# Three gatings moved forward in VectorE's order and two squares moved between the tiles' signs, in a cross-attention and mixture-of-experts kernel

## The chip, the cores and the metric

The kernel runs on one core of a Trainium2 chip. The metric is the device time of one execution in microseconds, as the median of several executions; the times of the profile are microseconds from the start of the profiled span.

## What is computed

For each of 16 examples of 256 tokens and width 256 the reference adds a cross-attention over 77 context rows and then a mixture of experts, each behind a layer norm. The attention has 16 heads and uses sparsemax in place of softmax.

```python
x = x + xattn(layernorm(x), ctx, ctx, ...)
x = x + ffn(layernorm(x), ...)

# xattn, per head:
scores = einsum('bhqd,bhkd->bhqk', qh, kh) * scale
attn   = sparsemax(scores)             # max(scores - tau, 0), sums to 1
out    = einsum('bhqk,bhkd->bhqd', attn, vh) ... @ Wo + bo

# ffn:
_, idx = top_k(logits + lb_bias, 2);  w = sigmoid(sel_logits); w = w / (sum(w) + 1e-6)
hidden     = square(relu(einsum('nd,ehd->neh', xf, w1)))       # 8 experts
expert_out = einsum('neh,edh->ned', hidden, w2)
moe_out    = einsum('ned,ne->nd', expert_out, we)
shared     = square(relu(x @ cfc.T)) @ cproj.T
```

## The kernel before

The kernel is a software pipeline over examples. Each engine runs 19 turns, `b` from 0 to 18, and in turn `b` it works on four examples at four depths: *new* (example b: norm, queries, scores, first estimate of tau), *mid* (example b-1: the remaining rounds on tau), *late* (example b-2: attention product, output projection, second norm, routing) and *old* (example b-3: the experts). Turns 3 to 15 have all four; turn 16 has no new example, turn 17 only late and old, turn 18 only old. In turns 0 to 2 nothing is old. The order of the work inside a turn is written out by hand for each engine in its function `turn`. All engines wait on semaphores, and each runs its instructions strictly in the order written.

**The experts (old).** Nine of them, the shared one first. For the i-th, TensorE's `layer1` (L807) writes `h_ps` with eight matmuls; VectorE's `old_gates` (L1072), called as `gates(i)`, multiplies the rectified result by the square root of the routing weight into `g` (ScalarE does it for i = 0); ScalarE's `old_square` (L577), called as `square(i)`, squares `g` into `hid`; TensorE's `layer2` (L820) accumulates it into `y_ps`. `h_ps`, `g` and `hid` are double buffers: `layer1(i)` waits until gating i-2 is done, `gates(i)` waits for `layer1(i)` and for square i-2, and `layer2(i)` waits for square i.

**The rounds (new and mid).** A round r on tau is: GpSimd subtracts tau from the scores, one tile of 128 tokens at a time (L335, `over`); ScalarE takes the signs (L526) and the relu (L528), in `sign_relu`; VectorE's `newton` folds the signs (L945, `fold_a`), sums the relu (L948), both for two tiles, then folds again (L954), sums (L958), takes a reciprocal (L960), a step (L962) and the new tau (L966). A function `between` is called after the second fold. Round 0 and 1 belong to the new example, where round 1's `newton` comes at the head of the next turn; rounds 2 and 3 are mid's. Round 3 has no signs.

**Routing (late).** TensorE's output projection (L780) feeds VectorE's `late_stats` (L1035 and the statistics), then GpSimd's `late_rstd` (L406, L408), ScalarE's `late_norm` (L481), TensorE's transposes (L788) and logits (L796). At a turn's end GpSimd's `late_pick` and `late_weight_roots` (L417, a power) make the roots of the weights `sw`. TensorE's `late_roots` (L665) transposes `sw`, which is TensorE's last step of the turn; its next is `layer1(0)` of the next turn. From there `sw` goes by ScalarE and two transfers into `sw_all`, which `gates(1)` of the next turn reads.

On GpSimd, behind round 0's tau of the new example, stand in this order: `subtract(b, p, 1, 0)` (waits for that tau), `late_pick`, `subtract(b, p, 1, 1)`, `mid_verdict`, `late_weight_roots`. On TensorE, around the change, stand `new_scores(b, 1)` (L732, waits until ScalarE has copied the first tile's scores, L514 and L516), `l2(2)`, the first product (L762, L771), `l1(4)`, `l2(3)`, `l1(5)`, the second product, the output projection, `l2(4)`, `l1(6)`, `l2(5)`, the transposes of x1n, `l1(7)`, the logits, `l2(6)`, `l1(8)`, `l2(7)`, `l2(8)`, `late_roots`.

Of the kernel before, what the change touches and what calls it, by code (L numbers as in the profile page):

```python
# [64 lines left out]
def xattn_moe_kernel(nc, x, ctx_in, wq, wk, wv, wo, bq, bk, bv, bo, gate_w, lb_bias, w1, w2, cfc, cproj,  # L65
# [4 lines left out]
    with ExitStack() as stack:  # L70
# [134 lines left out]
        def rt(r, t):  # L205

            return r * T + t + 1
# [248 lines left out]
        def _(act):  # L456
# [122 lines left out]
            def turn(b, p, q, new=False, mid=False, late=False, old=False, ahead=True):  # L579
                def square(i):  # L580
                    if old and i == 0:
                        old_shared(b - 3)
                    if old:
                        old_square(b - 3, i)

                def keys_on(i):
                    if b < 2:
                        i += PAIRS // 2 * b
                        pair_keys(i)
                        if i < PAIRS - 1:  # L590
                            pair_context(i + 1)

                if b == 0:
                    pair_context(0)
                    pair_keys(0)
                if new:
                    new_turned(b, 0)
                square(0)
                if new:
                    new_turned(b, 1)  # L600
                    new_queries(b)
                square(1)
                if mid:
                    sign_relu(b - 1, q, 2, 0)
                    sign_relu(b - 1, q, 2, 1)
                if new:
                    new_scores(b, p, 0)
                square(2)
                if new:
                    new_scores(b, p, 1)  # L610
                if b == 0:
                    pair_context(1)
                if b == 1:
                    keys_on(0)
                if late:
                    late_product(b - 2, 0)
                square(3)
                if mid:
                    sign_relu(b - 1, q, 3, 0)
                    sign_relu(b - 1, q, 3, 1)  # L620
                if late:
                    late_product(b - 2, 1)
                square(4)
                if new:
                    sign_relu(b, p, 0, 0)
                    keys_on(1)
                    sign_relu(b, p, 0, 1)
                    keys_on(2)
                square(5)
                if late:  # L630
                    late_norm(b - 2, p)
                if late:
                    late_turned(b - 2, p)
                if mid:
                    mid_attention(b - 1, 0)
                square(6)
                if late:
                    late_sigmoids(b - 2)
                if mid:
                    mid_attention(b - 1, 1)  # L640
                square(7)
                if new and ahead:
                    new_norm(b + 1, q)
                keys_on(3)
                if new:
                    sign_relu(b, p, 1, 0)
                square(8)
                if new:
                    sign_relu(b, p, 1, 1)
                if late:  # L650
                    late_roots(b - 2)
# [239 lines left out]
        def _(dve):  # L891
# [32 lines left out]
                dve.wait_ge(top_chain.sem, top_chain.at(b, 2 * t + 1))  # L924
                dve.tensor_reduce(top_sum[:, t], top8[:, t], AX.X, ALU.add).then_inc(top_chain.sem, 1)

            def newton(b, p, r, between, gap=None):

                n0 = 4 * r
                if r == COUNTS:  # L930
                    for t in range(T):
                        dve.wait_ge(relu_done.sem, relu_done.at(b, rt(r, t)))
                        dve.tensor_reduce(fsum[:, t * NH:(t + 1) * NH], over[:, p, t], AX.X, ALU.add  # L933
                                          ).then_inc(f_summed.sem, 1)
                    between()
                    dve.wait_ge(f_summed.sem, f_summed.at(b))
                    dve.scalar_tensor_tensor(step[:], fsum[:], -1.0, rden[:], ALU.add, ALU.mult
                                             ).then_inc(newton_chain.sem, 1)
                    dve.wait_ge(newton_chain.sem, newton_chain.at(b))
                    dve.scalar_tensor_tensor(flat(tau[:, p]), step[:], 2.0, flat(tau[:, p]), ALU.mult, ALU.add  # L940
                                             ).then_inc(tau_ready.sem, 1)
                    return
                for t in range(T):
                    dve.wait_ge(sign_done.sem, sign_done.at(b, rt(r, t)))
                    dve.tensor_tensor(fold_a[:, t], signs[:, p, t, :, 0:SW // 2], signs[:, p, t, :, SW // 2:], ALU.add  # L945
                                      ).then_inc(signs_folded.sem, 1)
                    dve.wait_ge(relu_done.sem, relu_done.at(b, rt(r, t)))
                    dve.tensor_reduce(fsum[:, t * NH:(t + 1) * NH], over[:, p, t], AX.X, ALU.add  # L948
                                      ).then_inc(f_summed.sem, 1)
                    if gap is not None and t == 0:  # L950
                        gap()
                dve.wait_ge(signs_folded.sem, signs_folded.at(b, rt(r, 1)))
                halves = fold_a[:].rearrange("p t h k -> p (t h) k")
                dve.tensor_tensor(fold_b[:], halves[:, :, 0:SW // 4], halves[:, :, SW // 4:], ALU.add  # L954
                                  ).then_inc(newton_chain.sem, 1)
                between()
                dve.wait_ge(newton_chain.sem, newton_chain.at(b, n0 + 1))
                dve.tensor_reduce(den[:, p], fold_b[:], AX.X, ALU.add).then_inc(newton_chain.sem, 1)  # L958
                dve.wait_ge(newton_chain.sem, newton_chain.at(b, n0 + 2))
                dve.reciprocal(rden[:], den[:, p]).then_inc(newton_chain.sem, 1)  # L960
                dve.wait_ge(newton_chain.sem, newton_chain.at(b, n0 + 3))
                dve.scalar_tensor_tensor(step[:], fsum[:], -1.0, rden[:], ALU.add, ALU.mult  # L962
                                         ).then_inc(newton_chain.sem, 1)
                dve.wait_ge(newton_chain.sem, newton_chain.at(b, n0 + 4))

                dve.scalar_tensor_tensor(flat(tau[:, p]), step[:], 2.0, flat(tau[:, p]), ALU.mult, ALU.add  # L966
                                         ).then_inc(tau_ready.sem, 1)
# [114 lines left out]
            def turn(b, p, q, new=False, mid=False, late=False, old=False, ahead=True):  # L1082
                def gates(i):
                    if old:
                        old_gates(b - 3, q, i)

                def newton_and_gates(stage, b, p, r, i, gap=None):
                    if stage:
                        newton(b, p, r, lambda: gates(i), gap)
                    else:  # L1090
                        gates(i)

                def values(i):
                    if b < 2:
                        pair_values(PAIRS // 2 * b + i)

                def verdict():
                    if late:
                        late_verdict(b - 2)

                if mid:
                    newton(b - 1, q, 1, verdict)
                else:
                    verdict()
                gates(1)
                if new and ahead:
                    new_stats(b + 1, q)
                if late:
                    late_settle(b - 2, p)
                newton_and_gates(mid, b - 1, q, 2, 2)  # L1110
                if new:
                    new_tau(b, p, 0)
                gates(3)
                if new:
                    new_tau(b, p, 1)
                values(0)
                newton_and_gates(mid, b - 1, q, 3, 4)
                if mid:
                    mid_magnitude(b - 1, q)
                if late:  # L1120
                    late_stats(b - 2, p)
                gates(5)
                newton_and_gates(new, b, p, 0, 6, lambda: values(1))
                values(2)
                gates(7)
                if mid:
                    mid_tolerance_sum(b - 1)
                if late:
                    late_gate(b - 2)
                values(3)  # L1130
                if late:
                    late_weights(b - 2)
                gates(8)
                if old:
                    old_finish(b - 3, q)
# [30 lines left out]
```

## Time and profile before

| | |
|---|---|
| device time, median of 3 runs | 932.8 us (932.24 to 937.07) |
| profiled execution, own time | 933.74 us |
| its span | 931.9 us |
| TensorE matmul busy | 800.4 us, 86% of the span |
| VectorE busy | 595.1 us, 64% |
| ScalarE busy | 573.0 us, 61% |
| GpSimd busy | 559.7 us, 60% |
| one turn with all four examples (503.73 to 554.10) | 50.37 us |

The busy shares are means over a ramp, thirteen like turns and a tail. The turns of 4 to 15 repeat to within some hundredths of a microsecond, so one of them, that of 503.73 to 554.10, is read in place of all. The ends of matmuls are modelled in the profile, and consecutive groups of eight overlap by a tenth or so in its rows.

### The profile page before, as it was taken

How to read it: one execution, taken by the hardware profiler on the slowest of the kernel's cores; microseconds unless marked ns; L12 is line 12 of the kernel's file. 1: busy time of each engine (PE TensorE's matmuls, PEld its weight loads, DVE VectorE, ACT ScalarE, POOL GpSimd, SP SyncE). 2: the span in 40 equal slices, each digit the busy share in tenths (PEclk: the TensorE clock that was granted, in tenths of full speed). 3: DMA queues.
4: the chain of work that ended last, by engine and by line, in shares of the span. 5: the costliest groups of instructions: out<-in, count | busy, mean ns of one | idle time of the engine just before them, and what ended most of it. 6: DMA issues, size and time to landing. Idle time of an engine off the chain costs nothing.

```text
span 931.9 us, 14502 instructions
## 1 busy us (share of the span) xinstructions
PE 800.4 (86%) x4800; PEld 655.1 (70%) x4800; DVE 595.1 (64%) x1691; ACT 573.0 (61%) x890; POOL 559.7 (60%) x605
## 2 busy tenths in 40 slices
PE   1846456989898999989999989899998999989998
PEld 1635345777787877877777778787786877768887
DVE  2479674867776767768586777676776858543221
ACT  1455665767768675767666776767576766543221
POOL 2448486766668585858676666858585867633010
PEclk9867777999999999999999999999999999999999
DMA  8200001020110201020102010020102010101010
GB/s 255 95 7 12 7 12 46 1 71 7 28 41 13 64 12 58 12 62 14 59 1 70 8 36 34 13 64 12 58 12 62 4 58 1 58 1 58 1 57 11
DMA packets 37355, 34.84 MB, mean 37 GB/s; under 512 B 23153, under 2 KB 34078, under 8 KB 35230
## 3 DMA queue, kind: packets, MB, share of 16 engines
q1 hardware_dynamic: 34934, 28.88, 11.1%
q0 software_dynamic: 1248, 4.73, 1.5%
q8 instruction: 38, 0.62, 0.3%
q10 hardware_dynamic: 1096, 0.29, 0.2%
q14 instruction: 39, 0.32, 0.1%
HBM read 28.30 MB, written 4.33 MB: 35 GB/s over the span
## 4 chain that ended last, share of the span: by engine, by line
PE 43%; POOL 17%; DVE 16%; issue 11%; ACT 9%; DMA 4%; ACTq 0%; POOLq 0%; DVEq 0%
PE h_ps L807 13%; PE y_ps L820 12%; POOL over L335 8%; PE m_ps L771 5%; POOL sw L417 4%; ACT signs L526 4%; PE s_ps L762 4%; PE m_ps L780 3%; DVE g L1072 3%; DMA sw_all<-sw_scratch 3%; DVE fsum L948 3%; PE m_ps L715 2%; DVE fold_a L945 2%; ACT over L528 2%; ACT hid L577 2%
## 5 line engine op out<-in xcount | busy, mean ns | idle before, releaser
L335 POOL TENSOR_TENSOR over<-S,tau 128x1232 f32<-128x1232 f32 x128 | 286.9, 2253 | 227.8 <-DVE tau L966 225.3
L820 PE MATMUL y_ps<-w_sb,hid 128*128 128x256 f32 x1152 | 280.4, 387 | 29.3 <-ACT hid L577 29.3
L807 PE MATMUL h_ps<-x1nT,w_sb 128*128 128x256 f32 x1152 | 277.5, 384 | 0.0
L820 PEld LDWEIGHTS y_ps<-w_sb,hid 128*128 128x128 f32 x1152 | 212.6, 191 | 72.6 <-ACT hid L577 44.6
L807 PEld LDWEIGHTS h_ps<-x1nT,w_sb 128*128 128x128 f32 x1152 | 216.7, 192 | 31.0 <-issue 3.0
L528 ACT ACTIVATE over<-over 128x1232 f32<-128x1232 f32 x128 | 155.5, 1228 | 3.0
L948 DVE TENSOR_REDUCE fsum<-over 128x16 f32<-128x1232 f32 x96 | 137.2, 1429 | 18.7 <-ACT over L528 18.5
L1072 DVE SCALAR_TENSOR_TENSOR g<-h_ps,sw_all 128x512 f32<-128x512 f32 x128 | 87.6, 685 | 81.2 <-DMA sw_all<-sw_scratch 43.7
L577 ACT ACTIVATE hid<-g 128x512 f32<-128x512 f32 x144 | 89.7, 623 | 64.7 <-DVE g L1072 64.2
L526 ACT ACTIVATE signs<-over 128x1232 bf16<-128x1232 f32 x96 | 117.3, 1222 | 3.6 <-POOL over L335 3.5
L922 DVE MAX8 top<-S 128x8 f32<-128x77 f32 x512 | 74.7, 223 | 12.4 <-ACT S L516 12.4
L542 ACT ACTIVATE attnT<-s_ps 128x512 f32<-128x512 f32 x64 | 34.9, 595 | 70.9 <-PE s_ps L762 70.9
L945 DVE TENSOR_TENSOR fold_a<-signs 128x640 bf16<-128x640 bf16 x96 | 61.9, 644 | 24.7 <-ACT signs L526 24.7
L335 POOL TENSOR_TENSOR attn<-S,tau 128x1232 f32<-128x1232 f32 x32 | 71.6, 2258 | 8.2 <-PE s_ps L762 7.5
L732 PE MATMUL s_ps<-k_diag,qT 64*128 64x308 f32 (+1 forms) x320 | 56.5, 430 | 15.1 <-ACT S L516 13.4
L732 PEld LDWEIGHTS s_ps<-k_diag,qT 64*128 64x128 f32 x320 | 43.4, 202 | 32.7 <-issue 24.2
L933 DVE TENSOR_REDUCE fsum<-over 128x16 f32<-128x1232 f32 x32 | 44.5, 1431 | 11.9 <-ACT over L528 11.1
L771 PE MATMUL m_ps<-attnT,v_block 128*32 128x128 f32 (+1 forms) x1088 | 47.1, 284 | 2.6 <-ACT attnT L542 1.7
L1035 DVE TENSOR_TENSOR x<-m_ps,xb 128x256 f32<-128x256 f32 x32 | 13.6, 425 | 55.6 <-PE m_ps L780 55.6
L417 POOL TENSOR_TENSOR sw<-wnorm,half_pow 128x16 f32<-128x16 f32 x16 | 46.9, 2930 | 1.3
L1080 DVE TENSOR_TENSOR wk_sb<-y_ps,x 128x256 f32<-128x256 f32 x32 | 12.1, 420 | 51.8 <-PE y_ps L820 51.8
L771 PEld LDWEIGHTS m_ps<-attnT,v_block 128*32 128x32 f32 (+1 forms) x1088 | 34.4, 110 | 14.9 <-ACT attnT L542 10.7
(103 smaller groups left out, 935.0 us busy)
## 6 DMA issues: line engine op xcount, KB each, us to landing
sw_all<-sw_scratch SPq DMA_DIRECT2D x16, 1024.0 KB, 5.3
x_sb<-in_x SPq DMA_DIRECT2D x16, 256.0 KB, 2.7
w_sb<-in_w POOLq DMA_DIRECT2D x2, 2048.0 KB, 12.1
out_y<-wk_sb SPq DMA_DIRECT2D x16, 256.0 KB, 5.6
sw_all<-in_ctx SPq DMA_DIRECT2D x1, 1078.0 KB
v_block<-v_all SPq DMA_DIRECT2D x56, 9.6 KB
wk_sb<-in_wk SPq DMA_DIRECT2D x1, 256.0 KB
wv_sb<-in_wv SPq DMA_DIRECT2D x1, 256.0 KB
```

Of the source, the lines that this page charges most:

```text
L335: return pool.tensor_tensor(dst, S[:, p, t], tau[:, p, t].rearrange("p (h o) -> p h o", o=1).broadcast_to([P, NH, NK]), ALU.subtract)
L417: pool.tensor_tensor(sw[:].rearrange("p t e -> p (t e)"), wnorm[:].rearrange("p t e -> p (t e)"), half_pow[:], ALU.pow).then_inc(sw_ready. ...
L526: act.activation(signs[:, p, t, :, 0:NK], over[:, p, t], ACT.Sign).then_inc(sign_done.sem, 1)
L528: act.activation(over[:, p, t], over[:, p, t], ACT.Relu).then_inc(relu_done.sem, 1)
L577: act.activation(hid[:, i % 2], g[:, i % 2], ACT.Square).then_inc(hid_ready.sem, 1)
L732: last = pe.matmul(s_ps[:, bank, col * NK:(col + n) * NK], qT[rows, c, t * P:(t + 1) * P], k_diag[rows, c, h0:h0 + n, :].rearrange("p h k ...
L771: last = pe.matmul(m_ps[32 * quad:32 * quad + 32, t, half * P:(half + 1) * P], v_block[0:rows, m % RING, BLOCKS.index((c, a)), :], attnT[0 ...
L807: last = pe.matmul(h_ps[:, i % 2, c, :], w1_sb[:, e, k, c * P:(c + 1) * P], x1nT[:, p, k, :], start=(k == 0), stop=(k == KC - 1))
L820: last = pe.matmul(y_ps[:, t, :], hid[:, i % 2, c, t * P:(t + 1) * P], w2_sb[:, e, c, :], start=(i == 0 and t == 0 and c == 0), stop=(i == ...
L945: dve.tensor_tensor(fold_a[:, t], signs[:, p, t, :, 0:SW // 2], signs[:, p, t, :, SW // 2:], ALU.add).then_inc(signs_folded.sem, 1)
L948: dve.tensor_reduce(fsum[:, t * NH:(t + 1) * NH], over[:, p, t], AX.X, ALU.add).then_inc(f_summed.sem, 1)
L1072: dve.scalar_tensor_tensor(g[:, i % 2], h_ps[:, i % 2], 0.0, sw_all[:, p, e:e + 1, :].broadcast_to([P, KC, TOK]), ALU.max, ALU.mult).then_ ...
```

## The change

VectorE: `gates(2)` and `gates(6)` no longer run inside `newton` of round 2 and round 0 (behind `fold_b`), but ahead of its first instruction; `gates(5)` runs ahead of `late_stats` rather than behind it; `gates(4)` keeps its place inside round 3. ScalarE: `square(2)` moves from behind the copy of the first tile's scores to between `sign_relu` of the two tiles of round 2, and `square(5)` from behind both tiles of round 0 to between them. No instruction is added or removed, and no data changes.

```diff
@@ ScalarE, turn
                 square(1)
                 if mid:
                     sign_relu(b - 1, q, 2, 0)
+                square(2)
+                if mid:
                     sign_relu(b - 1, q, 2, 1)
                 if new:
                     new_scores(b, p, 0)
-                square(2)
@@
                 if new:
                     sign_relu(b, p, 0, 0)
                     keys_on(1)
+                square(5)
+                if new:
                     sign_relu(b, p, 0, 1)
                     keys_on(2)
-                square(5)
                 if late:
                     late_norm(b - 2, p)
@@ VectorE, newton
-                between()
+                if between is not None:
+                    between()
@@ VectorE, turn
-                newton_and_gates(mid, b - 1, q, 2, 2)
+                gates(2)
+                if mid:
+                    newton(b - 1, q, 2)
@@
-                newton_and_gates(mid, b - 1, q, 3, 4)
+                if mid:
+                    newton(b - 1, q, 3, lambda: gates(4))
+                else:
+                    gates(4)
                 if mid:
                     mid_magnitude(b - 1, q)
+                gates(5)
                 if late:
                     late_stats(b - 2, p)
-                gates(5)
-                newton_and_gates(new, b, p, 0, 6, lambda: values(1))
+                gates(6)
+                if new:
+                    newton(b, p, 0, gap=lambda: values(1))
```

## Rows read from the trace of the kernel before

**Rows 1.** The page: busy time of TensorE and VectorE, and the granted clock

```profile
PE 800.4 (86%) x4800; PEld 655.1 (70%) x4800; DVE 595.1 (64%) x1691; ACT 573.0 (61%) x890; POOL 559.7 (60%) x605
PEclk9867777999999999999999999999999999999999
```

**Rows 2.** One turn's window: busy by engine, granted clock, DMA share, GB/s

```profile
503.73:554.10 50.37, 46.68 (x291) 38.48 (x291) 35.91 (x106) 35.06 (x54) 34.71 (x38) 1.00 0.14 36
```

**Rows 3.** The chain that ended last, 543 to 554: start, length, what

```profile
543.67 0.20 DVE tau L966
...
543.94 2.25 POOL over L335
...
550.72 2.94 POOL sw L417
```

**Rows 4.** TensorE's timeline, same turn: start, length, what, [idle before <-releaser]

```profile
518.49 1.60 PE L732 MATMUL s_ps<-k_diag,qT 64*128 64x308 f32 x10 [0.15 <-ACT S L516]
520.39 1.99 PE L820 MATMUL y_ps<-w_sb,hid 128*128 128x256 f32 x8 [0.29 <-ACT hid L577]
...
536.38 1.89 PE L807 MATMUL h_ps<-x1nT,w_sb 128*128 128x256 f32 x8
539.17 1.99 PE L820 MATMUL y_ps<-w_sb,hid 128*128 128x256 f32 x8 [0.90 <-ACT hid L577]
541.00 0.63 PE L788 MATMUL m_ps<-ident,wv_sb 128*128 128x128 f32 x4
...
550.03 1.99 PE L820 MATMUL y_ps<-w_sb,hid 128*128 128x256 f32 x8 [0.60 <-ACT hid L577]
553.70 0.38 PE L665 MATMUL m_ps<-ident,sw 128*8 128x128 f32 x2 [1.67 <-POOL sw L417]
```

**Rows 5.** VectorE's timeline, same turn

```profile
513.77 0.49 DVE L945 TENSOR_TENSOR fold_a<-signs 128x640 bf16<-128x640 bf16 x1 [0.76 <-ACT signs L526]
...
536.79 0.68 DVE L1072 SCALAR_TENSOR_TENSOR g<-h_ps,sw_all 128x512 f32<-128x512 f32 x1
537.39 0.82 DVE L945 TENSOR_TENSOR fold_a<-signs 128x640 bf16<-128x640 bf16 x1
...
541.62 0.68 DVE L1072 SCALAR_TENSOR_TENSOR g<-h_ps,sw_all 128x512 f32<-128x512 f32 x1
542.22 0.80 DVE L958 TENSOR_REDUCE den<-fold_b 128x32 f32<-128x640 bf16 x1
```

**Rows 6.** ScalarE's timeline, same turn

```profile
517.11 0.92 ACT L514 ACTIVATE S<-s_ps 128x924 f32<-128x924 f32 x1
...
538.50 0.61 ACT L577 ACTIVATE hid<-g 128x512 f32<-128x512 f32 x1
540.04 1.09 ACT L481 ACTIVATE wv_sb<-x,f_shift,f_rstd 128x256 f32<-128x256 f32 x2 [0.93 <-POOL f_shift L408]
```

**Rows 7.** GpSimd's timeline, same turn

```profile
533.40 4.46 POOL L335 TENSOR_TENSOR attn<-S,tau 128x1232 f32<-128x1232 f32 x2
...
539.96 1.28 POOL L330 TENSOR_TENSOR xb<-x_sb,bo_sb 128x512 f32<-128x512 f32 x1
```

**Rows 8.** TensorE's timeline, turn 16

```profile
805.59 0.55 PE L665 MATMUL m_ps<-ident,sw 128*8 128x128 f32 x2 [2.33 <-POOL sw L417]
805.93 3.45 PE L807 MATMUL h_ps<-x1nT,w_sb 128*128 128x256 f32 x8
...
822.47 3.55 PE L820 MATMUL y_ps<-w_sb,hid 128*128 128x256 f32 x8 [4.08 <-ACT hid L577]
```

**Rows 9.** VectorE's timeline, turn 16

```profile
815.67 0.52 DVE L945 TENSOR_TENSOR fold_a<-signs 128x640 bf16<-128x640 bf16 x1 [1.82 <-ACT signs L526]
...
821.07 0.68 DVE L1072 SCALAR_TENSOR_TENSOR g<-h_ps,sw_all 128x512 f32<-128x512 f32 x1
```

**Rows 10.** A window of turn 16: granted clock is the third figure from the end

```profile
806.00:806.50 0.50, 0.50 (x3) 0.41 (x3) 0.50 (x2) 0.33 (x1) 0.00 (x0) 0.50 0.00 0
```

**Rows 11.** The line of the weights' roots, turns 2 to 15: count, durations, who waited

```profile
L417 POOL TENSOR_TENSOR sw<-wnorm,half_pow x14: 2930/2930/2936, 145.4 to 802.6; 128x16 f32<-128x16 f32 x14
```

More of the change, by code:

```diff
@@ L925, in new_tau, with newton @@
                 dve.tensor_reduce(top_sum[:, t], top8[:, t], AX.X, ALU.add).then_inc(top_chain.sem, 1)
-            def newton(b, p, r, between, gap=None):
+            def newton(b, p, r, between=None, gap=None):
                 n0 = 4 * r
@@ L1085, in gates @@
                         old_gates(b - 3, q, i)
[L1087 to L1091, printed above, removed]
                 def values(i):
```

## The prediction, written before the changed kernel ran

> **What bounds the kernel.** I read the page first, then the waits by engine, then one turn's window, the chain of waits through it, and the timeline of each engine. TensorE is the busiest engine at 86%, with VectorE at 64%, and its clock stands at full from slice 7 on [rows 1]. That alone would say "TensorE bound". One turn of the thirteen full ones tells more: of 50.37 us TensorE's matmuls fill 46.68 [rows 2], so 3.7 us of a turn are waits, and the turn can only get shorter where one of those ends earlier. They are these: 0.15 us ahead of the second tile's scores, 0.29 ahead of layer2(2), 0.90 ahead of layer2(5), 0.60 ahead of layer2(8), and 1.67 ahead of the transposes of the weights' roots [rows 4]. The last is the one that sets the turn. The next turn's layer1(0) stands behind those transposes, and the chain reaches them from VectorE's tau of round 0 (543.67), by GpSimd's subtraction that starts at 543.94, the pick, the second subtraction, and the root that starts at 550.72 [rows 3]. A slot recovered on TensorE ahead of that wait only makes the wait longer. So the period of a turn is: from the transposes to whatever releases round 0's tau, then 9.8 us (543.87 to 553.70) of GpSimd that the change doesn't touch.
>
> What releases that tau now? VectorE goes without a pause from the statistics behind the output projection through gates(5) at 536.79, fold_a at 537.39 and, with gates(6) at 541.62 in the middle, to the tau [rows 5]. layer1(6), which gates(6) needs, starts at 536.38 and lasts 1.89, so it is done at 538.27 [rows 4]. Where gates(6) stands today that is 3.3 us early. Where the change puts it, at VectorE's 536.8, it is 1.5 us too late.
>
> **Gating 6 (the step that decides).** After the change VectorE runs out of the statistics at 536.79, has no gates(5) there any more (0.60 us less, 536.79 to 537.39), and stands at gates(6) until layer1(6) is done. With the shift of 0.19 worked out below, that is 538.46; VectorE starts some 0.04 later, and fold_a follows 0.60 after that, at 539.10, in place of 537.39: 1.71 late. Two things come back: gates(6) is gone from behind fold_b, 0.60 (541.62 to 542.22), and the first fold_a, now stretched to 0.82 where the one at 513.77 takes 0.49, gets back about 0.34 [rows 5]. It starts at 537.39 while GpSimd's subtraction still runs until 537.86 [rows 7], and at 539.10 that is over. Against this, the second fold_a would now start at 540.85, and GpSimd's xb runs 539.96 to 541.24 [rows 7]; it starts a little earlier in the new order, so I charge 0.1. Sum: 1.71 - 0.60 - 0.34 + 0.1 = 0.87 us later for the tau. Queued behind the waiting instruction are the whole of round 0's `newton`, gates(7), the late gating and the weights; GpSimd's subtract(1, 0) waits for the tau, and behind it in GpSimd's order stand the pick, the root and so TensorE's next turn. Bounds: 0.6 (no shift, no collision of the second fold) to 1.3 (shift, both folds stretched).
>
> That VectorE and GpSimd block one another is also what the Trainium skill says ("SBUF — State Buffer", section "Who interferes with whom"): a VectorE instruction with two SBUF inputs holds off a GpSimd one that reads SBUF, and the other way round. The 0.82 beside the 0.49 agrees. By that rule a collision of fold_a and xb costs at most what is left of xb, some 0.3 us in place of my 0.1; the total would be 2.6 us higher over thirteen turns.
>
> **Gating 2 and square 2.** gates(2) needs layer1(2), done long before round 2's second half; VectorE idles 0.76 us ahead of fold_a at 513.77 and the gating takes 0.60 of its time [rows 5], so it costs nothing on VectorE as long as ScalarE's signs remain the later. On ScalarE square(2) now stands ahead of the second tile's sign and relu and so delays these and the copy of the scores by its 0.53 us, from 517.11 [rows 6]. VectorE's tau of round 2 gains 0.60 and loses 0.53: nothing. TensorE's new_scores(b, 1), at 518.49 by that very copy, goes to 519.02; layer2(2) follows 1.56 later at 520.58, its wait of 0.29 gone, in place of 520.39 [rows 4]. So TensorE is 0.19 late from there, and has no gap until layer1(6) in which to make it up. Bounds 0 to 0.5.
>
> **Gating 5 and square 5.** gates(5) moves into a pause of 3.1 us in which VectorE waits for the output projection; layer1(5) is done by then. The statistics start no later, so it is free there. ScalarE squares between the tiles at about 536.4, not 538.50 [rows 6], and TensorE's layer2(5) doesn't wait its 0.90. Yet x1n is ready only once GpSimd's shift is (540.04, ScalarE waits for it [rows 6]), and the transposes of x1n, at 541.00 now, could start at about 540.5 at the earliest: at best half of the 0.90 survives, and all of it goes into the wait for the roots, which grows. Worth 0 in a full turn.
>
> **The wait grows.** layer2(8) hangs on square(8), which hangs on the pick and on GpSimd's subtraction, and moves by 0.1; the root moves by 0.87. So TensorE's wait of 1.67 becomes about 2.4. In turn 16 a wait of 2.33 was followed by half clock: the two transposes and eight matmuls of layer1(0) took 0.55 and 3.45 [rows 8] where 0.38 and 1.89 are usual [rows 4], at a granted clock of 0.50, that is 1.2 GHz [rows 10]. The wait of 1.67 never had this effect in twelve turns. A fall costs 0.17 + 1.56 = 1.7 us, straight onto the turn. Bounds 0 falls and 13 (22 us). The nearest row says it can happen, but it is a single one, and 2.4 barely exceeds it; I take two, 3.4 us. The Trainium skill ("TensorE: Matmul & The Clock Gate", "What's actually happening") says that the monitor of activity runs freely and is not reset by the kernel; by that, which of the waits is caught differs from turn to turn and from run to run, and no run here shows it yet.
>
> **Turn 16.** Nothing is new there, so no round 0. Here gates(2) fits into the idle 1.82 ahead of fold_a, where it now waits until 821.07 [rows 9]; TensorE's layer2(2) lost 4.08 to it and then ran at half clock, 3.55 for 1.99 [rows 8]. Both go: 5.6 us. x1n then comes later than TensorE, since GpSimd starts its attention subtraction after round 3's tau and gains only some 4 to 5 there. I take 5.1, bounds 4.0 and 5.7. Turns 17 and 18: 0.1. Turns 0 to 2 have no old example, nothing moves.
>
> **Sum.** The root line shows fourteen instances, turns 2 to 15 [rows 11]; thirteen of these turns, 3 to 15, have both a round 0 and a gating 6. 13 x 0.87 = 11.3; less 5.2 for the tail; plus 3.4 for two falls: +9.5 us. The span goes from 931.9 to 941.4, the profiled time from 933.74 to 943.2; that execution lay 0.9 above the median, so the median goes from 932.8 to 942.3.
>
> **Rivals.**
> 1. *The clock falls in most turns.* Same mechanism, but seven to thirteen falls: 938.9 + 1.7 x 7 to 13, that is 951 to 961. For it: the only wait near 2.4 fell. Against it: one row. 0.15.
> 2. *The loss is smaller than the tail's gain or equal to it.* If the tau is only 0.4 us late, 13 x 0.4 = 5.2 cancels turn 16; up to 0.75 it stays within 0.5%. It would need layer1(6) to end earlier, by 0.5 us, than a TensorE without a gap from 520 to 538 can make it. 933 to 937. 0.13.
> 3. *TensorE bounds the turn (faster).* Then the waits at layer2(2) and layer2(5) are what counts: 1.0 us per turn less, 13 us, plus the tail's 5.2: 915; halved because x1n is late, 921. It decides if GpSimd's root is ready when TensorE gets there, that is if the tau is not late at all; today TensorE waits 1.67 for it in each turn, which speaks against it. 0.07.
>
> The forecast, zero to six falls with the tau 0.6 to 1.3 late, has 0.65: from 13 x 0.6 - 5.7 to 13 x 1.3 - 4 with up to six falls, most of it between 937 and 950.
>
> **Range and chances.** 936 to 957 leaves out rival 3, most of rival 2 and the end of rival 1. A measurement of this kernel can tell about 0.5%, 4.7 us, from no change: faster 0.07, same 0.14 (rival 2 and a little of the forecast), slower 0.79.
>
> **What the new profile should show.** A wait of VectorE on layer1(6) ahead of g L1072, about 1.5 us in each full turn (536.98 to 538.50 by the old times), thirteen times. Period of a turn 51.2, with no falls. TensorE's wait ahead of L665 at about 2.4, and none ahead of layer2(5). The chain enters VectorE by `h_ps` L807, no longer by the statistics. In turn 16 the 4.08 us wait is gone. The forecast is wrong if that wait on layer1(6) stays under 1 us, if the wait ahead of L665 does not grow, or, in size, if the granted clock is at half ahead of many turns.

## The result, and the profile after

The changed kernel takes 941.65 us in the median of six runs (939.76 to 943.96), the kernel before 932.92 us in its six (931.62 to 937.07). The ratio is 1.0088, with a 95% interval of 1.0065 to 1.0112: slower by 0.9%. The profiled execution took 943.53 us, with a span of 941.7. The forecast was 942.3.

The page of the changed kernel, its busy times, clock and three groups (busy and mean ns, then the idle time ahead and who ended it):

```profile
PE 798.5 (85%) x4800; PEld 652.5 (69%) x4800; DVE 602.3 (64%) x1691; ACT 580.0 (62%) x890; POOL 551.7 (59%) x605
...
PEclk9967677999999999999999999999999999999999
...
L335 POOL TENSOR_TENSOR over<-S,tau 128x1232 f32<-128x1232 f32 x128 | 286.6, 2250 | 251.5 <-DVE tau L969 248.9
L822 PE MATMUL y_ps<-w_sb,hid 128*128 128x256 f32 x1152 | 277.4, 384 | 19.2 <-ACT hid L577 19.2
...
L1075 DVE SCALAR_TENSOR_TENSOR g<-h_ps,sw_all 128x512 f32<-128x512 f32 x128 | 87.9, 687 | 121.3 <-PE h_ps L809 72.2
```

Busy times and the clock tell little [rows 1]: the busy sums of VectorE and ScalarE are 7 us larger and GpSimd's is 8 us smaller, but the mean durations in these three groups are within 3 ns of the old ones, and the granted clock differs in two slices of the start by a tenth. The idle times tell more. Before, the gatings had this group:

```profile
L1072 DVE SCALAR_TENSOR_TENSOR g<-h_ps,sw_all 128x512 f32<-128x512 f32 x128 | 87.6, 685 | 81.2 <-DMA sw_all<-sw_scratch 43.7 <-PE h_ps L807 37.5
```

Their wait for layer1 rose from 37.5 to 72.2 us. Thirteen waits of 1.43 us, one in each turn from 3 to 15 and all ahead of gating 6, make 18.6 of the 34.7 added; most of the rest stands ahead of gating 2 and is put down to layer1 by the profile, though it is another pause (taken up below). TensorE waited 19.2 us for the squares where it had waited 29.3, and GpSimd 248.9 us for the taus where it had waited 225.3. The lines have moved by one to three since the version before: L1072 is L1075 here, L665 L667, L732 L734, L807 L809, L820 L822.

A full turn of the changed kernel on TensorE, from one transposition of the roots (512.94) to the next; it answers to [rows 4]:

```profile
512.94 0.38 PE L667 MATMUL m_ps<-ident,sw 128*8 128x128 f32 x2 [2.32 <-POOL sw L417]
...
528.65 1.60 PE L734 MATMUL s_ps<-k_diag,qT 64*128 64x308 f32 x10 [0.72 <-ACT S L516]
530.18 1.99 PE L822 MATMUL y_ps<-w_sb,hid 128*128 128x256 f32 x8
...
546.17 1.89 PE L809 MATMUL h_ps<-x1nT,w_sb 128*128 128x256 f32 x8
547.90 1.89 PE L822 MATMUL y_ps<-w_sb,hid 128*128 128x256 f32 x8
549.97 0.93 PE L790 MATMUL m_ps<-ident,wv_sb 128*128 128x128 f32 x4 [0.18 <-ACT wv_sb L481]
...
559.89 1.99 PE L822 MATMUL y_ps<-w_sb,hid 128*128 128x256 f32 x8 [1.19 <-ACT hid L577]
```

The waits ahead of layer2(2) (0.29) and layer2(5) (0.90) are gone. In their place stand 0.72 ahead of the scores (0.15 before), 0.18 ahead of the transposes of x1n (none before), 1.19 ahead of layer2(8) (0.60 before) and 2.32 ahead of the roots' transposes (1.67 before). In turn 16 the 4.08 us wait is gone; the longest that is left there is 1.27.

VectorE in the same turn, answering to [rows 5]:

```profile
523.62 0.69 DVE L1075 SCALAR_TENSOR_TENSOR g<-h_ps,sw_all 128x512 f32<-128x512 f32 x1 [0.82 <-issue]
...
546.52 0.14 DVE L906 TENSOR_SCALAR f_veps<-f_mv 128x1 f32<-128x1 f32 x1
548.10 0.69 DVE L1075 SCALAR_TENSOR_TENSOR g<-h_ps,sw_all 128x512 f32<-128x512 f32 x1 [1.43 <-PE h_ps L809]
548.71 0.48 DVE L947 TENSOR_TENSOR fold_a<-signs 128x640 bf16<-128x640 bf16 x1
...
552.20 0.48 DVE L956 TENSOR_TENSOR fold_b<-fold_a 128x640 bf16<-128x640 bf16 x1
552.71 0.82 DVE L961 TENSOR_REDUCE den<-fold_b 128x32 f32<-128x640 bf16 x1
...
554.18 0.19 DVE L969 SCALAR_TENSOR_TENSOR tau<-step,tau 128x32 f32<-128x32 f32 x1
```

The first row is gating 2, which comes back below. Behind the statistics the reader sees a bubble of 1.43 us where there was none, a first fold of 0.48 in place of 0.82, and no gating between fold_b and den.

The chain of waits in that turn passes through it:

```profile
542.68 1.92 PE m_ps L782 x8
544.61 1.73 PE y_ps L822 x8
546.33 1.74 PE h_ps L809 x8
548.08 0.02 issue
548.10 0.69 DVE g L1075
```

Before, the chain left TensorE at the output projection and ran on through VectorE's statistics:

```profile
532.89 1.94 PE m_ps L780 x8
...
534.85 0.42 DVE x L1035
```

Now it stays on TensorE for two more groups, until layer1(6), and enters VectorE by gating 6.

The starts of the roots (L417) divide the span into turns. This table is worked out from these rows of each trace (the turn shown above is one of 51.26):

| us | before | after |
|---|---|---|
| first root (end of turn 2) | 145.40 | 146.02 |
| turn 3 | 52.83 | 53.56 |
| usual full turn | 50.36 | 51.22 |
| turns out of the usual | 50.46 | 52.61, 52.76, 51.65, 51.32 |
| thirteen turns together | 657.21 | 671.72 |
| last of these roots to the end of the span | 129.29 | 123.96 |

So the thirteen turns gave 14.5 us away, the end won 5.3 back, and the start was 0.6 later: 9.8 us, which is the difference of the spans (941.7 and 931.9).

### The profile page after: what moved, and what is told of

Its sections match the earlier page's. It is cut to its first block, busy times and chain, and to the rows that moved or that the text cites. A ratio compares the mean times of both kernels' runs of the same rounds, so it can differ in the third digit from the quotient of the medians.

```text
span 941.7 us, 14502 instructions
## 1 busy us (share of the span) xinstructions
PE 798.5 (85%) x4800; PEld 652.5 (69%) x4800; DVE 602.3 (64%) x1691; ACT 580.0 (62%) x890; POOL 551.7 (59%) x605
## 4 chain that ended last, share of the span: by engine, by line
PE 45%; POOL 17%; DVE 13%; issue 9%; ACT 8%; DMA 7%; ACTq 0%; DVEq 0%; POOLq 0%
PE h_ps L809 13%; PE y_ps L822 13%; POOL over L335 8%; PE m_ps L773 5%; DMA sw_all<-sw_scratch 5%; DVE fsum L950 4%; POOL sw L417 4%; PE s_ps L764 4%; ACT signs L526 3%; PE s_ps L734 3%; PE m_ps L782 3%; PE m_ps L717 2%; DVE fold_a L947 2%; DVE g L1075 2%; ACT S L514 2%
## 5 line engine op out<-in xcount | busy, mean ns | idle before, releaser
L335 POOL TENSOR_TENSOR over<-S,tau 128x1232 f32<-128x1232 f32 x128 | 286.6, 2250 | 251.5 <-DVE tau L969 248.9
L822 PE MATMUL y_ps<-w_sb,hid 128*128 128x256 f32 x1152 | 277.4, 384 | 19.2 <-ACT hid L577 19.2
L809 PE MATMUL h_ps<-x1nT,w_sb 128*128 128x256 f32 x1152 | 277.2, 384 | 0.0
L822 PEld LDWEIGHTS y_ps<-w_sb,hid 128*128 128x128 f32 x1152 | 212.9, 190 | 56.5 <-ACT hid L577 26.0
L809 PEld LDWEIGHTS h_ps<-x1nT,w_sb 128*128 128x128 f32 x1152 | 216.2, 192 | 30.8 <-issue 3.0
L1075 DVE SCALAR_TENSOR_TENSOR g<-h_ps,sw_all 128x512 f32<-128x512 f32 x128 | 87.9, 687 | 121.3 <-PE h_ps L809 72.2
L950 DVE TENSOR_REDUCE fsum<-over 128x16 f32<-128x1232 f32 x96 | 137.3, 1430 | 18.8 <-ACT over L528 18.6
L734 PE MATMUL s_ps<-k_diag,qT 64*128 64x308 f32 (+1 forms) x320 | 54.9, 420 | 24.9 <-ACT S L516 23.2
L947 DVE TENSOR_TENSOR fold_a<-signs 128x640 bf16<-128x640 bf16 x96 | 64.4, 670 | 11.2 <-ACT signs L526 10.6
L734 PEld LDWEIGHTS s_ps<-k_diag,qT 64*128 64x128 f32 x320 | 42.3, 196 | 42.1 <-issue 33.6
L514 ACT ACTIVATE S<-s_ps 128x924 f32<-128x924 f32 x32 | 29.8, 932 | 33.5 <-PE s_ps L734 33.5
L773 PE MATMUL m_ps<-attnT,v_block 128*32 128x128 f32 x1088 | 47.1, 283 | 3.0 <-ACT attnT L542 2.0
L417 POOL TENSOR_TENSOR sw<-wnorm,half_pow 128x16 f32<-128x16 f32 x16 | 46.9, 2930 | 1.3
L773 PEld LDWEIGHTS m_ps<-attnT,v_block 128*32 128x32 f32 x1088 | 34.4, 110 | 15.2 <-ACT attnT L542 11.0
L717 PE MATMUL m_ps<-xnT,wq_sb 128*128 128x256 f32 x128 | 35.9, 431 | 9.7 <-ACT xnT L501 9.7
```

The costliest lines, as they stand in the source:

```text
L335: return pool.tensor_tensor(dst, S[:, p, t], tau[:, p, t].rearrange("p (h o) -> p h o", o=1).broadcast_to([P, NH, NK]), ALU.subtract)
L417: pool.tensor_tensor(sw[:].rearrange("p t e -> p (t e)"), wnorm[:].rearrange("p t e -> p (t e)"), half_pow[:], ALU.pow).then_inc(sw_ready. ...
L734: last = pe.matmul(s_ps[:, bank, col * NK:(col + n) * NK], qT[rows, c, t * P:(t + 1) * P], k_diag[rows, c, h0:h0 + n, :].rearrange("p h k ...
L773: last = pe.matmul(m_ps[32 * quad:32 * quad + 32, t, half * P:(half + 1) * P], v_block[0:rows, m % RING, BLOCKS.index((c, a)), :], attnT[0 ...
L809: last = pe.matmul(h_ps[:, i % 2, c, :], w1_sb[:, e, k, c * P:(c + 1) * P], x1nT[:, p, k, :], start=(k == 0), stop=(k == KC - 1))
L822: last = pe.matmul(y_ps[:, t, :], hid[:, i % 2, c, t * P:(t + 1) * P], w2_sb[:, e, c, :], start=(i == 0 and t == 0 and c == 0), stop=(i == ...
```

## The experiments

The ratios are to the kernel before, run beside each experiment on the same chip; its median was 932 to 935 us each time. Experiments on different chips are best compared by their ratios. "Period" is the usual distance of two roots in the trace.

**1. Gating 6 back in its old place.** All else as changed.

```diff
-                gates(6)
                 if new:
-                    newton(b, p, 0, gap=lambda: values(1))
+                    newton(b, p, 0, lambda: gates(6), lambda: values(1))
+                else:
+                    gates(6)
```

> The changed kernel with gates(6) alone put back inside round 0's newton, behind the second fold. Theory (VectorE's wait on layer1(6) ahead of round 0 sets the loss): that wait and the 2.3 us wait ahead of the roots' transposes go back to 1.7, the period of a full turn to 50.3, turn 16 keeps its gain: 927 to 929 us. Rival A (the delay of TensorE by square(2), 0.2 us a turn, passes to the turn): 930 to 931. Rival B (the loss comes from the squares between the tiles' signs): stays at 940 to 942.

928.82 us, ratio 0.9962 (0.9932 to 0.9993), by the ratios some 12 us less than the changed kernel; the wait ahead of the roots' transposes is 1.66 again. One gating's place turns a gain into a loss. The period is 50.42, not 50.3, so a little of the squares' delay does pass to the turn. VectorE in this kernel:

```profile
535.40 1.35 DVE L947 TENSOR_TENSOR fold_a<-signs 128x640 bf16<-128x640 bf16 x1
...
539.77 0.47 DVE L956 TENSOR_TENSOR fold_b<-fold_a 128x640 bf16<-128x640 bf16 x1
540.17 0.68 DVE L1075 SCALAR_TENSOR_TENSOR g<-h_ps,sw_all 128x512 f32<-128x512 f32 x1
```

The first fold comes 0.45 us sooner in its turn (gating 5's 0.6 out of the way, the statistics 0.15 later), and takes 0.5 us longer than the 0.82 of [rows 5]: it ends 0.34 us behind GpSimd's subtraction. The same shows below in the kernel with gating 5 alone.

**2. Gating 6 alone.** The kernel before, with this in place of the call with `newton_and_gates(new, b, p, 0, 6, ...)`:

```diff
+                gates(6)
+                if new:
+                    newton(b, p, 0, lambda: None, lambda: values(1))
```

> The kernel before with one edit, gates(6) ahead of round 0's newton. Theory: VectorE waits about 0.9 us for layer1(6) there, tau 0.7 us later, 13 turns give 9, turn 16 gains nothing, and the longer wait ahead of the roots' transposes may bring up to three falls of the clock at 1.7: 941 to 946 us. Rival B (loss from the squares): 932 to 934. If TensorE bounded the turn: 933.

947.90 us, ratio 1.0136 (1.0101 to 1.0171), 1.9 above the expected range. VectorE waits 0.83 us for layer1(6). The period is 51.04, and 51.04 - 50.36 = 0.68 is the 0.7 expected for the tau. It is 0.18 below the 51.22 of the changed kernel, where layer1(6) starts about as much later in its turn; square 2's delay is the only edit there that holds TensorE up ahead of layer1(6). The time is out of the range since more came on top than the falls of the clock that were allowed for. In the trace these are three full turns of 51.49 to 52.60 (one with half clock, two in which the weights for gating 1 came late), 1.2 us at the end and 0.9 at the start. Without the gain of turn 16 this single edit is worse than the whole change.

**3. Gating 2 and square 2 alone.**

```diff
                     sign_relu(b - 1, q, 2, 0)
+                square(2)
+                if mid:
                     sign_relu(b - 1, q, 2, 1)
                 if new:
                     new_scores(b, p, 0)
-                square(2)
@@
-                newton_and_gates(mid, b - 1, q, 2, 2)
+                gates(2)
+                if mid:
+                    newton(b - 1, q, 2, lambda: None)
```

> The kernel before with gates(2) ahead of round 2's newton and square(2) between the tiles' signs, nothing else. Theory: turn 16 alone gains 5.1, and the 0.2 us by which TensorE comes later in a full turn is swallowed by GpSimd's subtraction, which holds VectorE's first fold of round 0 until 537.9 anyway: 927 to 929 us. Rival A (the 0.2 passes to the turn, 13 times): 930 to 931. Rival B (the squares between the signs make the loss): 938 or more.

932.55 us, ratio 1.0000 (0.9967 to 1.0033): a miss. In its trace the last root is 124.64 from the end, so the gain there is real (4.65); the usual turn is 50.42, 0.06 longer. But four turns of thirteen took 50.5 to 50.8, where the kernel before had one of 50.46, and the thirteen are 1.7 us longer in sum. In the longest of them ScalarE shows why:

```profile
413.30 1.23 ACT L528 ACTIVATE over<-over 128x1232 f32<-128x1232 f32 x1
414.80 0.63 ACT L577 ACTIVATE hid<-g 128x512 f32<-128x512 f32 x1 [0.27 <-DVE g L1073]
415.34 1.22 ACT L526 ACTIVATE signs<-over 128x1232 bf16<-128x1232 f32 x1
```

The square stands between the signs and waits 0.27 us for its gating; the second tile's signs, the scores' copy and TensorE wait with it. VectorE's pause ahead of this gating (0.82 in the rows of the changed kernel) is 0.82 to 0.84 in most turns here too, but 1.13 in this one (turn 8) and 1.16 in turn 13. Turns 8 and 13 have the same longer pauses in the traces of the changed kernel and of 1, 4 and 7, and are longer than usual in all of them. Why these two turns, no run shows. That leaves a gain of 2.9 us in the trace and 0.8 in the medians, with an interval of 3 either way: how much of the difference between the two is chance of the runs stays open.

**4. layer1(6) earlier.** The changed kernel with one swap on TensorE, whose inputs allow it (gating 4 is long done).

```diff
-                l2(4)
                 l1(6)
+                l2(4)
                 l2(5)
```

> The changed kernel with one edit on TensorE: layer1(6) ahead of layer2(4) in place of behind it, so that it ends 1.7 us earlier. Theory: VectorE no longer waits at gates(6), the tau of round 0 comes 0.6 us earlier than in the kernel before (the gating's 0.6 out of the chain), period 49.8, 919 to 923 us. Rival C (a gating ahead of the round costs its own time wherever layer1(6) ends, or GpSimd and VectorE hold each other up): 932 to 942.

922.75 us, ratio 0.9879 (0.9846 to 0.9913). VectorE in a turn of this kernel:

```profile
378.34 0.68 DVE L1075 SCALAR_TENSOR_TENSOR g<-h_ps,sw_all 128x512 f32<-128x512 f32 x1
378.93 0.75 DVE L947 TENSOR_TENSOR fold_a<-signs 128x640 bf16<-128x640 bf16 x1
...
384.68 0.19 DVE L969 SCALAR_TENSOR_TENSOR tau<-step,tau 128x32 f32<-128x32 f32 x1
```

No wait at the gating, period 49.95: 0.41 below that of before, which is what the gating's 0.60 less the 0.19 by which TensorE comes late would give, and not the 49.8 expected. The place that the change chose costs only because layer1(6) ends later than VectorE comes to it; with that wait taken away the same place gains. The median says this less surely than the period does. Of the 11.4 us by which this trace is shorter than that of before, 5.1 lie ahead of the first root, where the order is that of the changed kernel; 1.8 lie in the thirteen turns, one of which took 53.13, and 4.6 at the end.

**5. Gating 5 and square 5 alone.** `gates(5)` above `late_stats`, `square(5)` between the signs of round 0, the rest as before.

> The kernel before with gates(5) ahead of the statistics and square(5) between the tiles' signs, nothing else. Theory: VectorE comes to round 0's first fold 0.6 us earlier, but GpSimd's subtraction holds that fold until 537.9 as before, so the tau, the period of 50.36 and the 1.67 us wait ahead of the roots' transposes stay; TensorE's 0.9 us wait ahead of layer2(5) is gone and reappears further on: 932 to 934 us. Rival (TensorE bounds the turn, so the 0.9 counts in 13 turns): 921 to 924. If the fold were not held: 925.

933.67 us, ratio 1.0001 (0.9979 to 1.0024), period 50.33: nothing. The wait of 0.9 ahead of layer2(5) is gone, but it only moved. On TensorE, here and, in the last row, before:

```profile
541.70 0.93 PE L789 MATMUL m_ps<-ident,wv_sb 128*128 128x128 f32 x4 [0.70 <-ACT wv_sb L481]
542.47 1.89 PE L808 MATMUL h_ps<-x1nT,w_sb 128*128 128x256 f32 x8
```

```profile
541.46 1.89 PE L807 MATMUL h_ps<-x1nT,w_sb 128*128 128x256 f32 x8
```

The turn's transposes of the roots are at 504.36 here and at 503.35 before, so layer1(7) starts 38.11 us behind them in both: nothing of the 0.9 gets past the transposes of x1n. So this run does not test the rival in which TensorE bounds the turn, as the expectation meant it to; 7 does. GpSimd and VectorE:

```profile
534.41 4.46 POOL L335 TENSOR_TENSOR attn<-S,tau 128x1232 f32<-128x1232 f32 x2
```

```profile
537.80 1.42 DVE L946 TENSOR_TENSOR fold_a<-signs 128x640 bf16<-128x640 bf16 x1
```

The 0.60 us that leave VectorE's order come back as a fold of 1.42 in place of 0.82, which ends 0.35 behind the subtraction.

**6. The suspected wait made longer.** The changed kernel with `gates(7)` behind `gates(6)`, ahead of round 0.

> The changed kernel with gates(7) moved ahead of round 0's newton as well, the suspected wait made longer. Theory: VectorE waits for layer1(7), which ends 4.6 us later than layer1(6); gates(7) was not in the chain to the tau, so its 0.6 comes on top: the tau 4.6 us later (548.7 to 553.3 for the first fold), the period 55.8, 1001 us without more falls of the clock, and up to 13 x 1.7 more where TensorE's waits, now near 6 us at layer2(8), bring the half clock in every turn: 1000 to 1023. Rival (VectorE's waits ahead of round 0 are swallowed up to some slack): under 980.

1008.39 us, ratio 1.0797 (1.0751 to 1.0844), inside the range. VectorE has a second wait, on layer1(7):

```profile
527.43 0.69 DVE L1075 SCALAR_TENSOR_TENSOR g<-h_ps,sw_all 128x512 f32<-128x512 f32 x1 [1.43 <-PE h_ps L809]
532.00 0.69 DVE L1075 SCALAR_TENSOR_TENSOR g<-h_ps,sw_all 128x512 f32<-128x512 f32 x1 [3.87 <-PE h_ps L809]
```

and TensorE a long one, after which layer2(8) runs at half clock:

```profile
543.77 3.66 PE L822 MATMUL y_ps<-w_sb,hid 128*128 128x256 f32 x8 [5.75 <-ACT hid L577]
548.09 0.38 PE L667 MATMUL m_ps<-ident,sw 128*8 128x128 f32 x2 [0.66 <-POOL sw L417]
```

Two turns took 55.8, as worked out without a fall of the clock, nearly all others 56.6. The wait for the roots, 2.32 in the changed kernel and 0.66 here, takes up what the slow layer2(8) costs TensorE. What is left comes another way: VectorE waits for layer2(8) before it goes on to round 1, and in the turn that begins at 548.09 layer2(0) waits 0.59 for VectorE's copy of the unsettled count, as it did not in the changed kernel:

```profile
553.27 1.97 PE L822 MATMUL y_ps<-w_sb,hid 128*128 128x256 f32 x8 [0.59 <-DVE unsettled_count L990]
```

Ahead of the two turns of 55.8 the clock came back a little sooner, layer2(8) took 3.38 and 3.52 us, and layer2(0) did not wait.

**7. Gating 6 behind the tau.** The changed kernel with `gates(6)` after round 0's `newton`.

> The changed kernel with gates(6) behind round 0's tau in place of ahead of its newton. Theory: the gating's 0.6 us leaves the chain to the tau without a wait taking its place, period 49.8 to 49.9, wait ahead of the roots' transposes about 1.2: 920 to 924 us, as with layer1(6) put earlier. Rival (square(6) and layer2(6) come late and hold TensorE up, by 0.6 or more a turn): 928 to 932.

924.47 us, ratio 0.9905 (0.9872 to 0.9938), period 49.98, the wait for the roots 0.85 (expected: 49.8 to 49.9, and 1.2). The chain to the tau loses the gating without a wait taking its place. Layer2(6) now waits 0.56 for its square, and TensorE comes to the roots' transposes 49.13 us after those of the turn before (49.98 - 0.85), where it came after 48.76 in experiment 1 (50.42 - 1.66). So TensorE's order became 0.37 us longer and the turn 0.44 us shorter: TensorE's order does not bound it. As in 4, the period says more than the median: 4.8 of the 10.2 us by which this trace is shorter than that of before lie ahead of the first root.

**8. The roots earlier.** As 7, and:

```diff
@@ GpSimd, turn
+                if late:
+                    late_weight_roots(b - 2)
                 if new:
                     subtract(b, p, 1, 1)
                 if mid:
                     mid_verdict(b - 1)
-                if late:
-                    late_weight_roots(b - 2)
@@ ScalarE, turn
+                if late:
+                    late_roots(b - 2)
                 if new:
                     sign_relu(b, p, 1, 1)
-                if late:
-                    late_roots(b - 2)
```

> The one before it (gates(6) behind the tau), and on GpSimd the weights' roots ahead of the second tile's subtraction of round 1, on ScalarE the copy of the turned roots ahead of that tile's signs. Theory (the 9.8 us on GpSimd between tau and roots is what the turn waits for): 2.8 us leave that chain, TensorE's wait ahead of the roots' transposes vanishes, and the period falls until TensorE's order or round 1's tau bounds it, 48.3 to 49.3: 900 to 915 us. Rival (the delayed second tile makes round 1's tau and then round 2's signs late by as much): 920 to 930.

918.20 us, ratio 0.9848 (0.9811 to 0.9884), outside both ranges. The wait for the roots is gone, but the period is 50.10. TensorE waits elsewhere:

```profile
532.06 0.93 PE L790 MATMUL m_ps<-ident,wv_sb 128*128 128x128 f32 x4 [0.63 <-ACT wv_sb L481]
...
536.08 1.99 PE L822 MATMUL y_ps<-w_sb,hid 128*128 128x256 f32 x8 [0.56 <-ACT hid L577]
...
549.10 1.97 PE L822 MATMUL y_ps<-w_sb,hid 128*128 128x256 f32 x8 [0.91 <-DVE unsettled_count L990]
```

With the 9.8 us of GpSimd out of the way TensorE's order does bound the turn, and each of its waits counts now. Against 7 the usual turn lost 0.12; what the run won over it, it won outside the usual turn: no turn was lengthened (50.1 to 50.2 all but the first), and turn 3 began after a wait of 6.90 in place of 9.17.

**9. Both early.** As 8, with `gates(6)` ahead of round 0 and `l1(6)` ahead of `l2(4)` (as 4), and the verdict's copy between round 1's tiles: `newton(b - 1, q, 1, gap=verdict)`.

> Roots early on GpSimd and ScalarE as in the run before, gates(6) ahead of round 0 with layer1(6) ahead of layer2(4), and the copy of the unsettled count on VectorE between the tiles of round 1 in place of behind the second fold. Theory (with the roots out of the way TensorE's own order bounds the turn, and what is left are its waits, the last profile's 0.9 us at layer2(0) for the count and 0.6 at layer2(6) for gating 6): both go, period 48.4 to 49.0, 897 to 908 us. Rival (round 1's tau and round 2's signs on ScalarE bound the turn already): period stays at 50.1, 916 to 920.

914.79 us, ratio 0.9797 (0.9762 to 0.9832), period 49.53: between the expected range and the rival's. The 0.56 is gone. The 0.91 for the count became 0.65 for ScalarE's square 0:

```profile
544.12 1.99 PE L822 MATMUL y_ps<-w_sb,hid 128*128 128x256 f32 x8 [0.65 <-ACT hid L577]
```

That square stands behind the second tile's signs, which the early roots made late. The expectation had counted the wait as gone when only its first releaser was.

**10. Turn 16 only.** The kernel before, with gating 2 and square 2 moved only where nothing is new (`if not new: square(2)` between the tiles' signs, and `gates(2)` ahead of `newton` in that case).

> The kernel before, with gates(2) ahead of round 2's newton and square(2) between the tiles' signs only in turn 16, where nothing is new; the full turns keep the old order. Theory: the full turns stay at 50.36, the end after the last root of a full turn shortens from 129.3 to 124.6 us as in the other kernels with this edit: 928 to 929 us. Rival (the gain at the end is eaten elsewhere, as the time of the run with the edit in all turns suggests): 932 to 934.

928.88 us, ratio 0.9942 (0.9920 to 0.9964), period 50.33, the end 124.62: as expected. Beside 3 it says that in the full turns the second gating's new place takes back a part of what it gives in turn 16: 1.7 of 4.7 us in the trace of 3. By the two ratios, 1.0000 and 0.9942, it is some 5 us, give or take 4.

**11. The best.** As 9, with 10's condition on gating 2 and square 2.

> The fastest so far, with the second gating and square back in their old places in the turns with a new example (the moved order stays in turn 16). Theory: the copy of the first tile's scores comes 0.5 earlier, TensorE's wait of 0.67 ahead of the second tile's scores splits into 0.15 and 0.3 again, 0.2 us a turn: period 49.3, 911 to 914 us, and no turn lengthened by a square that waits for its gating. Rival (with the roots early, another wait takes the 0.2): no change, 914 to 916.

912.70 us, ratio 0.9779 (0.9745 to 0.9812), 2.2% faster than the kernel before. The period is 49.40, 0.13 less than in 9 (0.2 expected), and from turn 4 on no turn leaves 49.40 to 49.42. The intervals of 9 and 11 overlap, so the times alone don't tell the two apart.

## Why the prediction was right

**The turn is set by the chain through round 0's tau, not by TensorE's order.** Shown by 1 and 2 (the gating alone), by 4 and 7, which both shorten that chain and shorten the turn, and by 7 beside 1, where TensorE's order got longer and the turn shorter. 5 shows only that the two edits on gating 5 and square 5 are worth nothing.

**Gating 6 waits for layer1(6).** Forecast 1.5 us of wait, measured 1.43; forecast 0.87 for a turn, measured 51.22 - 50.36 = 0.86. The two parts also stand apart: 0.68 without the shift of TensorE (experiment 2), 0.18 for the shift, against 0.68 and 0.19 in the sum. The charge of 0.1 for a collision of the second fold wasn't needed (the fold took 0.48), nor was a larger one; but den starts 0.51 behind fold_b's start where gating 6 had started 0.40 behind it, and that 0.1 made up for it by chance. Experiment 4 takes the wait away by an earlier layer1(6), and the loss turns into a gain.

**Gating 2 and square 2.** On TensorE as forecast: 0.72 ahead of the scores, none ahead of layer2(2). That it costs VectorE nothing came out (round 2's tau is 0.1 later in its turn), but not as argued. The sum put the gating into the 0.76 us that VectorE idles ahead of the fold, as a wait for ScalarE's signs. In the changed kernel VectorE idles 0.82 us ahead of the gating itself, and the fold comes 0.87 later in its turn; with the gating gone from behind fold_b and shorter waits for ScalarE, round 2 makes this up. So the pause is VectorE's own. In the chain of waits it is filled with steps of VectorE's sequencer at L995 to L998, where `late_settle` reads the unsettled count into a register. The gating now ends at about the time at which ScalarE is ready for square 2 (the square starts at 524.34), so the square has next to no room, and waits whenever its gating is some tenths late (experiment 3). The sum left this out.

**Gating 5 and square 5: 0.** Right (experiment 5), and for one reason more than the two given: GpSimd's subtraction holds the first fold anyway. Of the 0.90, of which the sum let half survive at best, nothing survives.

**The end.** Forecast 5.2, measured 129.29 - 123.96 = 5.3, and 4.7 in 3 and 10.

**The grown wait and the clock.** Forecast 2.4 us and two falls worth 3.4. Measured 2.32, and one fall. Of the turns out of the usual, that from 306.43 had it:

```profile
306.43:359.20 52.77, 48.28 (x291) 39.40 (x292) 36.59 (x106) 35.56 (x54) 34.03 (x38) 0.97 0.13 34
...
308.00:309.00 1.00, 1.00 (x3) 0.46 (x2) 1.00 (x1) 0.00 (x0) 0.00 (x0) 0.50 0.03 8
```

The clock was granted at 0.50 (1.2 GHz) from within 307 to 311, and the turn took 1.5 us more than usual. The turn from 253.82 had full clock, and lost 1.4 us to another cause, a store of the turned roots that landed late:

```profile
254.64 2.56 DMA sw_scratch<-swT
257.21 5.49 DMA sw_all<-sw_scratch
```

In the profile of before such a store took 1.3 (from 554.52 to the spread's start at 555.83). The turns that begin at 410.40 and 666.63 are turns 8 and 13 of experiment 3's pause. It was 1.13 and 1.16 us, the weights came 0.26 late too in the second, and the scores came 0.09 and 0.43 late. So the term of 3.4 us had the right size by luck: 1.5 of it was the clock, 1.4 a late transfer, and 0.5 the square without room. The late transfer is no effect of the change: in the traces of 5 and 10, whose full turns have square 2 in its old place, one turn each took 51.09 and 51.22 with stores of 2.15 and 2.52 us. How often either came in the other runs of the changed kernel isn't recorded, and the median of 941.65 holds them as they fell.

## What to carry to other kernels

An instruction that is moved forward into an engine's idle time brings its own operand's wait with it: compare the time at which the engine would reach it with the time at which the producer ends, at the new place, before counting the gap as free. The wait that ends last in a turn decides what a change is worth; a recovered wait ahead of it only moves into it, and once it is gone another takes over with a releaser that stood hidden behind the first.

A turn of a pipeline that lacks one stage (turn 16 here) may want another order than the full ones: the same edit gained 4.7 us there and gave a part of them back in the thirteen others.

## What the hardware showed unexpectedly

**A wait for GpSimd can hide in a VectorE duration.** The same fold took 0.48, 0.82, 1.35 and 1.42 us, by how long GpSimd's instruction beside it still ran, with no idle time shown. In the changed kernel, at a turn's start on GpSimd and on VectorE:

```profile
509.95 2.93 POOL L417 TENSOR_TENSOR sw<-wnorm,half_pow 128x16 f32<-128x16 f32 x1
512.86 1.22 POOL L322 TENSOR_TENSOR k_diag<-kT,head_of 128x616 f32<-128x616 f32 x1
```

```profile
511.33 0.48 DVE L947 TENSOR_TENSOR fold_a<-signs 128x640 bf16<-128x640 bf16 x1
...
513.07 1.35 DVE L947 TENSOR_TENSOR fold_a<-signs 128x640 bf16<-128x640 bf16 x1
```

The second fold ends 0.34 behind k_diag (514.42 and 514.08); the first takes its usual 0.48 within the 2.93 us power. The Trainium skill ("SBUF — State Buffer", "SBUF: two separate sides") says that whichever instruction comes first holds the shared ports for its whole length. The fold beside k_diag agrees; the one beside the power, which also reads SBUF, does not, so not every GpSimd instruction holds VectorE up. Experiment 6 shows the other order. In its two turns of 55.8 the fold starts first, 0.15 and 0.01 us ahead of k_diag, and takes 0.48, and it is k_diag that takes 1.42 and 1.54 in place of 1.22.

**The clock after a wait of some 2.3 us was not the same each time.** TensorE waited 2.32 or 2.33 for the roots at thirteen places of the changed kernel, each followed by the same first matmuls, and the granted clock fell to half once; in experiment 2, again after one of thirteen such waits (2.31 or 2.32). Ahead of turn 16 the same wait stands in five more traces: the clock fell in the kernel before and in experiment 1, and not in 3, 5 and 10. After the waits of 1.67 it never fell, but that is no bound: in experiment 7 it fell to 0.50 between 791.5 and 792, after a wait of 1.56 ahead of layer2(6). The Trainium skill ("TensorE: Matmul & The Clock Gate", "What's actually happening") has the monitor run freely, not reset by the kernel; these rows agree with that.

**The start varies.** The first root came between 140.3 and 146.7 us in the traces of before, of the changed kernel and of 1 to 7 and 10, all of which have it in the same place of GpSimd's order; it came at 146.02 and 140.63 in the changed kernel and in experiment 7, whose orders are the same up to there. (In 8, 9 and 11 the root itself stands earlier, and came at 138.0 to 141.9.) This is more than many of the differences measured, and is why the turns of a trace told more than the medians. Its cause wasn't sought.
